# Skip term written by ScalarE into the PSUM banks that the turned sum adds onto, with a new order of the work and all sixteen rounds written out

## The reference

```
xr = layernorm(x) @ W_in ; xi, res = split(xr)
u  = silu(causal_conv4(xi) + conv_b)
dbc = u @ W_x -> delta_r (8), B (16), C (16)
delta = softplus(delta_r @ W_dt + b_dt) ; A = -exp(A_log)
h_t = exp(delta_t * A) * h_(t-1) + delta_t * B_t * u_t        # per channel and state
y_t = sum over the 16 states of h_t * C_t
y = (y + u * D) * silu(res) ; x = x + y @ W_out
z = layernorm(x) ; scores = z @ gate_w.T ; weights = softmax(top 2 scores)
x = x + sum over 8 experts e of weight[e] * (silu(z @ w1[e].T) @ w2[e].T)
```

## Time and profile before

| | |
|---|---|
| median of 3 runs | 1091.44 us (1090.85 to 1091.58) |
| the profiled execution | 1092.1 us, of which the span from the first to the last instruction is 1090.0 us |
| granted PE clock, mean over the span | 0.978 of full speed |
| PE, DVE, ACT, POOL busy | 1040.8, 1017.5, 907.1, 959.6 us |
| matmuls recorded for `skip_in` (L1747) | 128, busy 18.4 us, mean 291 ns |
| HBM traffic over the span | 76 GB/s |

### The profile page before, as it was taken

The page is one execution under the profiler, slowest core; times in us unless marked ns, Lnnn a source line. Parts: engine busy times, 40 slices in busy tenths (PEclk is TensorE's granted clock), DMA queues, the critical chain, the costliest instruction groups (busy, mean ns, idle before and its releaser), DMA issues.

```text
span 1090.0 us, 18707 instructions
## 1 busy us (share of the span) xinstructions
PE 1040.8 (95%) x6150; PEld 758.0 (70%) x6150; DVE 1017.5 (93%) x1057; ACT 907.1 (83%) x1379; POOL 959.6 (88%) x890
## 2 busy tenths in 40 slices
PE   7787789999999999999999999999999999989998
PEld 4445466677777777777776777777777776767776
DVE  5999999999999999999999999999999999999822
ACT  4987867988989999998989899899989989875533
POOL 4688886999999999999999999999999999799934
PEclk9698989999999999999999999999999999989999
DMA  5332111122040312204031311403130130320000
GB/s 202 137 127 77 71 48 79 59 108 78 1 158 28 127 59 103 82 9 173 3 126 58 126 58 40 145 0 126 58 136 39 66 109 0 137 87 11 11 8 14
DMA packets 37364, 84.12 MB, mean 77 GB/s; under 512 B 3320, under 2 KB 28208, under 8 KB 28976
## 3 DMA queue, kind: packets, MB, share of 16 engines
q1 hardware_dynamic: 36880, 83.06, 21.4%
q10 hardware_dynamic: 416, 0.30, 0.1%
HBM read 78.63 MB, written 4.72 MB: 76 GB/s over the span
## 4 chain that ended last, share of the span: by engine, by line
PE 83%; DVE 9%; issue 4%; ACT 3%; DMA 0%; POOL 0%; DVEq 0%; ACTq 0%; POOLq 0%
PE work L1829 19%; PE work L1806 18%; PE y_ps L1758 18%; PE work L1682 8%; DVE h L1258 6%; PE rows L1737 4%; PE work L1779 3%; PE work L1666 2%; PE work L1701 2%; PE rows L1829 2%; PE work L1692 2%; PE rows L1806 1%; DVE rows L1248 1%; PE y_ps L1747 1%; PE work L1727 1%
## 5 line engine op out<-in xcount | busy, mean ns | idle before, releaser
L551 POOL TENSOR_TENSOR h<-h,c_rows 128x1024 f32<-128x1024 f32 x256 | 599.9, 2364 | 53.5 <-DVE h L1258 53.2
L1258 DVE TENSOR_TENSOR_SCAN h<-dA,rows 128x1024 f32<-128x1024 f32 x256 | 579.0, 2276 | 1.1
L872 ACT ACTIVATE dA<-delta,a_neg 128x510 f32<-128x510 f32 x512 | 325.7, 707 | 7.9 <-DVE h L1258 4.4
L1248 DVE TENSOR_TENSOR rows<-du,rows 128x1024 f32<-128x1024 f32 x256 | 306.7, 1214 | 4.9 <-PE rows L1737 4.9
L1758 PEld LDWEIGHTS y_ps<-ident,h 128*128 128x128 f32 x2048 | 241.2, 144 | 62.3 <-issue 34.5
L1758 PE MATMUL y_ps<-ident,h 128*128 128x128 f32 x2048 | 270.0, 278 | 10.3 <-POOL h L551 10.3
L1829 PEld LDWEIGHTS work<-w,hid 128*128 128x128 f32 x1856 | 223.3, 193 | 34.5 <-ACT hid L906 18.9
L1806 PE MATMUL work<-x2T,w 128*128 128x512 f32 x474 | 240.2, 602 | 2.9 <-ACT u L790 2.3
L1829 PE MATMUL work<-w,hid 128*128 128x128 f32 x1856 | 229.1, 277 | 2.4 <-ACT hid L906 2.2
L906 ACT ACTIVATE hid<-work 128x512 f32<-128x512 f32 x237 | 139.3, 596 | 65.5 <-PE work L1806 63.7
L591 POOL TENSOR_TENSOR x<-x,weighted 128x512 f32<-128x512 f32 x127 | 161.9, 1274 | 19.6 <-DVE weighted L1340 19.2
(11 more groups left out here) (147 smaller groups left out, 941.7 us busy)
## 6 DMA issues: line engine op xcount, KB each, us to landing
c_rows<-c_dram SPq DMA_DIRECT2D x64, 1024.0 KB, 5.0
x_in<-in_x SPq DMA_DIRECT2D x16, 256.0 KB, 3.0
x_again<-in_x SPq DMA_DIRECT2D x16, 256.0 KB, 3.4
out<-x SPq DMA_DIRECT2D x15, 256.0 KB, 2.6
w<-in_w1T SPq DMA_DIRECT2D x1, 1024.0 KB, 4.8
w<-in_w2T SPq DMA_DIRECT2D x1, 1024.0 KB, 7.0
h<-in_conv_w SPq DMA_DIRECT2D x1, 512.0 KB, 4.9
c_dram<-bcd SPq DMA_DIRECT2D x16, 32.0 KB, 1.6
```

The costliest lines, as they stand in the source:

```text
L551: nc.gpsimd.tensor_tensor(at, at, c_rows[:, n, :].unsqueeze(1).broadcast_to([P, H, T]), ALU.mult).then_inc(c_used, 1)
L872: last = nc.scalar.activation(two_seqs(dA[:, n % RING, half, :])[:, :, 1:], two_seqs(delta[:, half, :])[:, :, 1:], ACT.Exp, scale=a_neg[:, ...
L1248: nc.vector.tensor_tensor(rows[:, n % 2], du[:, j.odd], rows[:, n % 2, H - 1, :].unsqueeze(1).broadcast_to([P, H, T]), ALU.mult).then_inc( ...
L1258: nc.vector.tensor_tensor_scan(h[:, n % RING].rearrange("p h t -> p (h t)"), dA[:, n % RING].rearrange("p h t -> p (h t)"), rows[:, n % 2] ...
```

## The change

The skip term no longer goes through PE. ACT writes `u * D` straight into the two banks of `work` (`skip(j, half)`), and the four transposes of `turn_y` add onto it (`onto=True`, no start flag). `skip_in` and the tile `ud` are gone; the first `sum_states` of a round carries the start flag and the wait for `copy_y` of the round before. `project_out` and `expert` set the start flag once for a bank instead of once for each 128 columns. `turn_y` waits for `skip` where it waited for the bank's last reader; `skip` now has that wait.

```diff
-            def skip(j):
+            def skip(j, half, *uses):
                 act.wait_ge(u_ready, j.count(H, H))
-                wait(act, skip_summed, j.count(1, 0))
-                for half in range(H):
-                    last = nc.scalar.activation(ud[:, half, :], u[:, j.odd, half, :], ACT.Copy,
-                                                scale=skip_w[:, half:half + 1])
-                last.then_inc(skip_ready, 1)
+                free(act, *uses)
+                nc.scalar.activation(bank(TURN_Y[half]), u[:, j.odd, half, :], ACT.Copy,
+                                     scale=skip_w[:, half:half + 1]).then_inc(skip_ready, 1)
...
-            def skip_in(j):
-                pe.wait_ge(skip_ready, j.count(1, 1))
-                wait(pe, yT_ready, j.count(1, 0))
-                for half in range(H):
-                    for b in range(TB):
-                        last = nc.tensor.matmul(y_ps[:, half, b, :], ud[:, half, b * P:(b + 1) * P], ident[:, :],
-                                                is_transpose=True, start=(b == 0), stop=False,
...
             def sum_states(j, n):
                 pe.wait_ge(c_used, j.count(NS, n + 1))
+                if n == 0:
+                    wait(pe, yT_ready, j.count(1, 0))
...
-            def turn_y(j, half, *uses):
+            def turn_y(j, half):
                 pe.wait_ge(yT_ready, j.count(1, 1))
-                free(*uses)
-                turn(work[:, TURN_Y[half], :], yT[:, half], y_turned)
+                pe.wait_ge(skip_ready, j.count(H, half + 1))
+                turn(work[:, TURN_Y[half], :], yT[:, half], y_turned, onto=True)
...
-    def run(eng, body, first, stages, stop):
-        loop_first = max(first, stages + 2)
-        pairs = (min(rounds, stop) - loop_first) // 2
-        with eng.Fori(0, pairs) as it:
-            body(Round(loop_first, it))
-            body(Round(loop_first + 1, it))
+    def run(body, first, stop):
+        for i in range(first, stop):
             body(Round(i))
...
-TURN_X2 = ("turn_x2", 1)
+TURN_X2 = ("turn_x2", 0)
-MOVED = {("expert", 1, 0): 5, ("expert", 1, 1): 3, ("expert", 1, 2): 2, ("expert", 1, 4): 3, ("expert", 1, 5): 2,
+MOVED = {("expert", 1, 0): 1, ("expert", 1, 1): 5, ("expert", 1, 2): 2, ("expert", 1, 3): 5, ("expert", 1, 4): 2,
```

More of the change, by code:

```diff
@@ L939, in round_ @@
                 hidden(four, 6, 1)
+                hidden(four, 7, 0)
                 copy_x2T(three)
+                hidden(four, 7, 1)
                 copy_xnT(i)
-                skip(one)
-                hidden(four, 7, 0)
-                hidden(four, 7, 1)
                 decay(one, 0)
@@ L1160, in _ @@
             hidden(r[12], 6, 1)
+            hidden(r[12], 7, 0)
             copy_x2T(r[13])
[L1162 to L1163 removed]
             hidden(r[12], 7, 1)
@@ L1656, in _, with turn @@
         def _(pe):
-            def free(*uses):
-                for s, j, per, more in uses:
-                    if there(j):
-                        pe.wait_ge(s, j.count(per, more))
-                        return
-            def turn(dst, src, signal):
+            def turn(dst, src, signal, onto=False):
                 for b in range(TB):
-                    last = nc.tensor.transpose(dst[:, b * P:(b + 1) * P], src[:, b, :], ident[:, :])
+                    last = nc.tensor.matmul(dst[:, b * P:(b + 1) * P], src[:, b, :], ident[:, :], is_transpose=True,
+                                            start=(b == 0 and not onto), stop=(b == TB - 1), skip_group_check=True)
                 last.then_inc(signal, 1)
@@ new lines, in round_ @@
+                sum_states(two, 14)
+                row_b(one, 2)
+                hidden(three, 0, 0, use_expert(four, 6), use_xnT(i), use_x2T(three))
+                hidden(three, 0, 1, use_expert(four, 7), use_scores(three))
+                sum_states(two, 15)
+                hidden(three, 1, 0, use_hid(three, 0, 0))
+                hidden(three, 1, 1, use_hid(three, 0, 1))
+                row_b(one, 3)
+                sum_states(one, 0)
+                turn_y(two, 0)
+                turn_y(two, 1)
@@ new lines, in round_ @@
+                row_b(one, 5)
+                convolve(i, 1, use_expert(three, 0), use_gated(two), use_hid(three, 1, 0), use_hid(three, 0, 0),
+                         use_expert(four, 6), use_xnT(i))
+                row_b(one, 6)
+                hidden(three, 2, 0, use_u(i, 0), use_gated(two), use_hid(three, 1, 1))
+                row_b(one, 7)
+                hidden(three, 2, 1, use_u(i, 1), use_expert(three, 0))
+                expert(three, 1, use_hid(three, 2, 0))
+                project_bcd(i, use_hid(three, 2, 1), use_u(i, 1))
@@ L1966, in lead_in @@
+                row_b(one, 11)
+                hidden(three, 4, 0, use_gate(i, 1), use_gate(i, 0), use_x1(two), use_expert(three, 2))
+                hidden(three, 4, 1, use_hid(three, 3, 1))
+                sum_states(one, 6)
             def lead_in():
```

1104 lines of the change are left out of this document (518 added, 586 removed).

## The result

The changed kernel takes 1138.38 us (median of 4 runs, 1129.59 to 1139.21), the kernel before 1091.51 us in the same series (1090.85 to 1092.08). The ratio is 1.0414, with a 95% interval of 1.0375 to 1.0453: slower by 4.1%, where 1% faster was forecast. The profiled execution took 1139.08 us, its span is 1137.3 us.

What follows compares the result with a forecast made beforehand. PE was taken to bound the middle and end, DVE 0.2 to 0.5 us a round behind. The last scan 6.4 us earlier and a tail 4.4 us shorter gave span 1079.2, median 1080.6 us; range 1075.5 to 1088.

Steps and rivals of the forecast that it cites:

- Point 4: New order in middle rounds: fewer ACT table changes and C's row loads moved on SP, together counted as nothing.
- Point 3: Loop edge on PE: writing out the rounds gains 0.20 us every second round, already inside the middle's sum.
- Point 1: Skip matmuls on PE: dropping groups of 0.87 us cuts PE's work in a middle round from 62.6 to 61.7 us.
- rival C: No change, 1090 to 1093 us, because PE has room after all; chance 0.05.
- Point 2: `turn_y` on PE waits for ACT's skip writes, 0.7 us a round; ten middle rounds still gain 3.0 us.
- Rival B: Slower: a late ACT makes PE's wait for the skip term 2.0 us a round, median 1099.7 us; chance 0.08.
- Point 5: Filling and draining: DVE's idle time shrinks by 2.0 us in each; one more `weight_expert` costs 0.6 us.
- Point 6: Tail: three hidden blocks and one expert move ahead of the last sum, shortening the end by 4.4 us.
- rival D: More gain than forecast: DVE's waits all but vanish, median 1076.3 us or a little less; chance 0.05.

Runs made afterwards that it cites:

- run 6: Changed kernel with C's row group 3 and the store of C's rows ahead of the load of x on SP, and `hidden`'s two waits exchanged: 1080.12 us.
- run 5: Kernel before with its loops written out and the two waits of `hidden` exchanged: 1084.59 us, ratio 0.9944.
- run 12: The kernel of run 5 measured again, side by side with run 11: 1084.51 us, ratio 0.9936.
- run 11: The kernel of run 6 measured again, side by side with run 12: 1082.38 us, ratio 0.9912.
- runs 1 to 3: Changed kernel, C's group 3 ahead of x's load: 1104.46 us; C's store too: 1103.39; kernel before, x's load ahead of C's loads: 1127.69.
- run 4: Kernel before with its loops written out and nothing else: 1109.60 us, ratio 1.0164.
- run 10: The kernel of run 6 with the skip term left out, ACT writing only 8 columns of each bank: 1079.85 us, ratio 0.9894.
- run 9: The kernel of run 6 with ACT writing the skip term in 8 pieces for each half: 1129.48 us, ratio 1.0346.
- run 7: Changed kernel, SP's order as it was, with only the two waits of `hidden` exchanged: 1108.70 us, ratio 1.0151.
- run 8: Kernel before, loops as they were, with the two waits of `hidden` exchanged: 1103.36 us, ratio 1.0108.

## Why the prediction was wrong

It had put two steps at nothing that cost the most: the place of C's loads on SP, and what straight code does to the table loads. With both losses removed the kernel takes 1080.1 and 1082.4 us (forecast 1080.6). The stages of the profiled executions of run 6 and of run 5, in which no skip term is moved, cut at the first scans of rounds 4 and 14 and at the last scan, stand beside the forecast's terms. The scans of run 6, then those of run 5:

```profile
269.46 2.27 DVE L1333 TENSOR_TENSOR_SCAN h<-dA,rows 128x1024 f32<-128x1024 f32 x1
...
897.41 2.28 DVE L1333 TENSOR_TENSOR_SCAN h<-dA,rows 128x1024 f32<-128x1024 f32 x1
...
1020.12 2.27 DVE L1333 TENSOR_TENSOR_SCAN h<-dA,rows 128x1024 f32<-128x1024 f32 x1
```

```profile
268.58 2.27 DVE L1262 TENSOR_TENSOR_SCAN h<-dA,rows 128x1024 f32<-128x1024 f32 x1
...
896.67 2.28 DVE L1262 TENSOR_TENSOR_SCAN h<-dA,rows 128x1024 f32<-128x1024 f32 x1
...
1019.39 2.29 DVE L1262 TENSOR_TENSOR_SCAN h<-dA,rows 128x1024 f32<-128x1024 f32 x1
```

| stage | forecast | both losses removed (run 6) | before, written out, exchanged (run 5) | as changed |
|---|---|---|---|---|
| to round 4's first scan | -2.0 | 269.46 - 272.94 = -3.5 | -4.4 | +3.3 |
| ten middle rounds | -3.0 | 627.95 - 629.50 = -1.6 | -1.4 | +43.0 |
| from there to the last scan | -2.0 + 0.6 | 122.71 - 124.95 = -2.2 | -2.2 | +2.0 |
| from the last scan to the end | -4.4 | 60.68 - 62.61 = -1.9 | -0.5 | -0.9 |
| span | -10.8 | -9.2 | -8.5 | +47.3 |

That the repaired kernel lands at the forecast is in good part luck. Its terms are off in both directions, and most of the gain is there in run 5 too, which keeps the skip matmuls and the old order: that kernel is 6.7 us under the kernel before, and 6.6 us in run 12. What the moved skip term and its order add is the distance of the pairs, 4.5 and 2.1 us. The only stage in which both pairs show a gain by it is the tail, 60.7 us in runs 6 and 11 against 62.1 and 62.0 in runs 5 and 12.

**Point 4, the step that failed first:** "On SP the loads of C's rows stand in other places; they land in 5.0 us against a round of 62.9 us, and the four groups are asked for as soon as their rows are used, so nothing. If one came late, POOL would stand for up to 5.0 us once." A load is asked for when SP comes to it, not when its buffer is free; it stood behind a load that waits for ACT till late in the round. The 5 us were right, the "once" was not: ten rounds, and runs 1 to 3 price it at 34 to 37 us. I had weighed the transfer's length and not what it was queued behind.

**Point 3, the loop:** "Gain: 0.20 us in every second round." That gain exists: in run 5, straight code without the table loads' fault, `project_out` starts 0.22 us behind the matmul that was the last at the loop's edge (548.37 to 548.59), where it was 0.42 in the earlier trace rows. Its middle rounds are 1.4 us shorter in ten (896.67 - 268.58 = 628.1 against 629.5), where 1.0 was forecast. The rest of that point put writing out the rounds at nothing, and this failed second: it turned around which of the two waits of `hidden` stands ahead of the table load, and the kernel before became 18.5 us slower by it in run 4, 25 us slower than with the waits exchanged (run 5). The trace of before had shown it: its own straight round 3 took 64.7 us and its looped rounds 62.9, and I put that down to filling.

**Point 1, the skip matmuls:** they went, but the round did not follow. PE's busy time is 0.4 us a round shorter in run 11 than in run 12; 0.87 was reckoned from their starts. Runs 11 and 12 have the same round with and without them. "So PE leads in the middle" doesn't fit that: in a round of run 6 DVE is busy for 62.51 of 62.79 us and PE for 62.20, and DVE's 0.5 us of idle before was all there was to win. In the middle the outcome is that of rival C, taking the matmuls away returned nothing; its reason was the other engine's list, not room that PE's rows had hidden.

**Point 2, the wait for the skip term:** forecast 0.7 us a round; PE's gap is 0.5 in the changed kernel, and it costs the round at most 0.22 (run 10). For what the writing takes, the upper price of 0.72 was taken; the mean of its rows is 0.68. Rival B's mechanism is real (run 9), but needs a later skip than there is.

**Point 5:** -3.5 and -2.2 where -2.0 and -1.4 were forecast, but not by its mechanism: run 5, with the skip groups and the old order, has -4.4 and -2.2, and run 12, the same kernel, -2.6 twice.

**Point 6, the tail:** from the last sum to PE's last matmul it is 1077.03 - 1027.99 = 49.0 us in run 6, as forecast:

```profile
1027.99 1.04 PE L1818 MATMUL y_ps<-ident,h 128*128 128x128 f32 x8
...
1077.03 0.61 PE L1882 MATMUL y_ps<-w,hid 128*128 128x128 f32 x4
```

But the end gained 1.9 us, not 4.4: the last sum now comes 7.9 us behind the last scan, where it was 5.5 (1032.91 - 1027.39). Between the two PE is without a gap in run 6, with two experts and hidden blocks among the sums, so part of the moved work was only put elsewhere.

In rival D, "-4.5" for ten rounds should be -5.0 by the prediction's own 0.5 us of idle a round; nothing hangs on it.

Open: why the changed kernel's executions scatter over 9.6 us and run 7's over 8.2, when those of run 6 scatter over 3.2. In both the fastest execution is the one with the highest granted clock (0.976 against 0.970, and 0.980 against 0.975 to 0.977); which of the two brings the other isn't shown.

## What to carry to other kernels

Price a moved DMA by what stands ahead of it in its queue and when that is released, not by its length: list for each issue of the in-order queue its wait and the time of its release. When waits change from registers to constants, or get another order, read which of them an activation carries and which stand ahead of a table load; where a kernel has the same body both looped and straight, compare the two rounds in the trace first. Where two engines are level, taking work from one can return almost nothing, as here, while a lateness that reaches the other can cost its full length, as in run 9. When a repaired kernel lands at the forecast, make the same repair in the kernel before as well, to see how much of the gain is the change's own.

## What the hardware showed

- The order of two waits in the source, the earlier of them long given, is worth 12 us in loops (run 8) and 25 us in straight code (1109.60 to 1084.59, runs 4 and 5), by the place of a 1.28 us table load.
- The Trainium skill (ScalarE: Activation LUTs, What ACT_TABLE_LOAD costs) counts 1380 ns of drain beside the load's 1283 ns. The traces agree with the load and show no drain in its place: in the changed kernel `skip` ends at 624.48 + 1.30 = 625.78, the next load begins at 625.79 and the decay behind it at 627.09, so a switch takes 1.3 us.
- ACT writes a 128x512 tile into PSUM in 0.68 us (mean of one, below, from the changed kernel), where the same operation took 0.72 into SBUF; back to back the busy time of 32 is 20.9 against 21.3 us.
- The store of 32 KB landed after 7.2 us behind 1.5 MB of loads issued in the 1.5 us before it, and after 1.6 us in the kernel before.
- Nothing in runs 5, 6, 11 or 12 shows a price of straight code: with all rounds written out, the ten middle ones ran at 62.8 us each.
- Waits on PE can be followed by a lower granted clock: in run 9 the four middle rounds at 0.95 to 0.97 took 0.7 to 2.6 us longer than the six at 1.00, with the same edit in all.

```profile
L922 ACT ACTIVATE work<-u,skip_w 128x512 f32<-128x512 f32 x32 | 20.9, 684 | 0.0
```
